# Four graph layers on one core: the slot's order changed at its seam and in its middle

## The reference

```python
x = _layernorm(x + L0(x, adj))   # conv1 -> relu -> conv2 (17 taps) -> + x -> relu
                                 # s = x @ w_se.T + b_se;  A = exp(-dist(s)) * adj
                                 # x_nmp = A @ relu(x @ w_msg.T + b_msg);  GRU(x_conv, x_nmp; x)
x = _layernorm(x + L1(x, adj))   # A = adj * sigmoid(q k^T / sqrt(128));  D^-1/2 A D^-1/2 X
x = _layernorm(x + L2(x, adj))   # tangent = artanh(|x|) x/|x|;  s = adj @ tangent
                                 # s * min(tanh|s|, 0.996) / |s|
x = _layernorm(x + L3(x, adj))   # relu(D^-1/2 (adj + I) D^-1/2 (x W^T + b) * mask)
```

## Time and profile before

| | |
|---|---|
| median of 3 runs | 797.41 us (796.39 to 798.12) |
| the profiled execution | 798.0 us, of which its span (first to last instruction) is 796.2 |
| busy share of the span | PE 90%, PEld 68%, DVE 79%, ACT 53%, POOL 17% |
| mean granted TensorE clock | 0.964 of full |
| one full slot | 45.30 us |

### The profile page before, as it was taken

One profiled execution on the slowest core, in us unless ns is written; L12 is line 12 of the kernel. 1 busy time (PEld: TensorE's weight loads), 2 busy tenths in 40 slices (PEclk: granted clock), 3 DMA queues, 4 the chain that ended last, 5 costly groups with the idle time before them and its releaser, 6 DMA issues.

```text
span 796.2 us, 12758 instructions
## 1 busy us (share of the span) xinstructions
PE 715.7 (90%) x3984; PEld 542.6 (68%) x3984; DVE 625.2 (79%) x2080; ACT 424.7 (53%) x881; POOL 135.3 (17%) x151
## 2 busy tenths in 40 slices
PE   3889999999999999999999999999999999998653
PEld 1766777777676877767776777767677776765531
DVE  7456788888878887888888888887888888876655
ACT  4164737556473755657373755647374655624431
POOL 0000111211122111211121121121121121111221
PEclk8889999999999999999999999999999999999776
DMA  5303241150605133060514224060423215101000
GB/s 198 119 14 129 97 158 68 57 169 14 224 14 171 66 108 116 23 215 13 193 44 162 75 66 158 13 224 13 171 66 122 102 45 192 54 14 54 0 14 27
DMA packets 46586, 75.33 MB, mean 95 GB/s; under 512 B 4065, under 2 KB 12769, under 8 KB 46433
## 3 DMA queue, kind: packets, MB, share of 16 engines
q1 hardware_dynamic: 46560, 75.02, 27.6%
HBM read 70.82 MB, written 4.19 MB: 94 GB/s over the span
## 4 chain that ended last, share of the span: by engine, by line
DVE 40%; PE 36%; issue 11%; ACT 9%; POOL 3%; DVEq 1%; DMA 0%; SPq 0%; ACTq 0%; POOLq 0%
PE K L1400 7%; DVE BIG L751 5%; PE C L1292 4%; PE CONV L1266 4%; DVE A L824 4%; PE F L1292 3%; ACT X L414 2%; DVE X L692 2%; POOL RSTD L336 2%; DVE Z L866 2%; ACT L553 2%; PE F L1353 2%; DVE FS L926 2%; DVE Z L991 2%; DVE ST L668 2%
## 5 line engine op out<-in xcount | busy, mean ns | idle before, releaser
L336 POOL TENSOR_TENSOR RSTD<-VEPS,POW 128x4 f32<-128x4 f32 x48 | 48.8, 1017 | 341.6 <-DVE VEPS L686 341.6
L1266 PE MATMUL CONV<-H1H,WH 128*128 128x256 f32 x288 | 85.6, 297 | 0.0
L1266 PE MATMUL CONV<-H1L,WH 128*128 128x256 f32 x288 | 81.4, 283 | 0.0
L1266 PE MATMUL CONV<-H1H,WL 128*128 128x256 f32 x288 | 81.2, 282 | 0.0
L1400 PE MATMUL K<-ADJR,FS 128*128 128x512 f32 x112 | 52.9, 617 | 10.1 <-DVE FS L926 10.1
L1364 PE MATMUL C<-QT,KT 128*128 128x512 f32 x128 | 61.6, 606 | 0.1
L1232 PEld LDWEIGHTS K<-XS,BIG 128*128 128x128 f32 x496 | 57.8, 192 | 1.3
L1232 PE MATMUL K<-XS,BIG 128*128 128x128 f32 x496 | 57.9, 275 | 0.0
L1232 PEld LDWEIGHTS K<-FX,ADJR 128*128 128x128 f32 x448 | 51.1, 192 | 9.9 <-issue 8.2
L1372 PE MATMUL F<-A,MSG 128*128 128x512 f32 x128 | 57.5, 592 | 0.0
L1266 PEld LDWEIGHTS CONV<-H1L,WH 128*128 128x128 f32 x288 | 55.2, 192 | 0.0
(11 more groups left out here) (251 smaller groups left out, 1932.1 us busy)
## 6 DMA issues: line engine op xcount, KB each, us to landing
ADJF<-in_adjT SPq DMA_DIRECT2D x16, 1024.0 KB, 5.3
ADJN<-in_adj SPq DMA_DIRECT2D x16, 1024.0 KB, 7.7
ADJM<-in_adjT SPq DMA_DIRECT2D x15, 1024.0 KB, 6.9
ADJR<-in_adjT SPq DMA_DIRECT2D x14, 1024.0 KB, 5.2
X_IN<-in_xT SPq DMA_DIRECT2D x16, 256.0 KB, 2.6
out<-OUT SPq DMA_DIRECT2D x16, 256.0 KB, 3.2
BIG<-in_weights SPq DMA_DIRECT2D x1, 1088.0 KB, 5.4
BIG<-in_weights SPq DMA_DIRECT2D x1, 576.0 KB, 8.7
```

Of the source, the lines that this page charges most:

```text
L336: nc.gpsimd.tensor_tensor(RSTD[:, row, :], VEPS[:, row, :], POW[:, 0, :], ALU.pow).then_inc(ev[f"ln{layer}_rstd"], 1)
L1266: last = mm(out, w[:, at_col + k * P:at_col + (k + 1) * P], h[:, k:k + PH], start=(k == 0 and i == 0), stop=(k == count - 1 and i == 2))
```

## The change

The distances get a bank each and move behind the transposes and the message rows; the bank list `DB` replaces the alternation, so F1 and K1 are used as well, and the transposes of Y move to F0, the message rows to K0.

```diff
+        DB = (C0, C1, F1, K1)
...
         def support_bank(n, c):
-            return (K0 if n["last"] else K1) if c < C // 2 or not n["drain"] else F0
+            return (K0 if n["last"] else K1) if c < C // 2 else F0 if n["drain"] else C1
...
             def support_norms(n):
                 for c in range(C):
-                    act.wait_ge(ev["agg2_done"], nth(finished(n, c), n["r"]))
+                    act.wait_ge(ev["agg2_done"], nth(c | 1, n["r"]))
...
+            def distances(n):
+                pe.wait_ge(ev["str_ready"], n["f"])
+                pe.wait_ge(ev["w_ready"], n["f_prev"])
+                pe.wait_ge(ev["gate_u"], n["f_prev"])
+                pe.wait_ge(ev["r_ready"], n["f_prev"])
+                pe.wait_ge(ev["res_scaled"], n["r_prev"])
+                for c in range(C):
+                    mm(DB[c][:, :], cols(STL, c), STR[:, :], start=True, stop=True).then_inc(ev["dist_done"], 1)
...
             def state_by_nodes(n):
                 pe.wait_ge(ev["y_ready"], n["m"])
-                pe.wait_ge(ev["d_kept"], n["m_prev"])
-                pe.wait_ge(ev["str_ready"], n["f"])
-                for c in range(C):
-                    last = nc.tensor.transpose(cols(K0, c), cols(Y, c), IDENT[:, :])
+                pe.wait_ge(ev["gate_t"], n["m"])
+                for c in range(C):
+                    last = nc.tensor.transpose(cols(F0, c), cols(Y, c), IDENT[:, :])
```

TensorE's `body` (in a full slot):

```diff
-                distances01(n)
                 if mid:
                     state_by_nodes(n)
-                distances23(n)
-                messages(n)
+                    messages(n)
+                distances(n)
...
                 if rear:
                     support(n)
+                summed_messages(n)
                 sum_taps(n)
                 odd_taps(8, EVEN).then_inc(ev["conv2_done"], 1)
-                summed_messages(n)
                 own_gates(n)
+                reset_gate_of_x(n)
+                if rear:
+                    last_aggregation(n)
                 if mid:
                     attention_degree(n)
-                reset_gate_of_x(n)
-                if rear:
-                    last_aggregation(n)
+                if rear:
+                    last_linear(n)
                 gates_of_messages(n)
-                if rear:
-                    last_linear(n)
                 reset_gate_of_conv(n)
```

More of the change, by code:

```diff
@@ L1177, in ending @@
                 degree_guard(c)
+                norm_guard(c)
                 ball_factor(c)
@@ L1256, in _ @@
             first_conv(1, 0)
-            factors(1, 0, 0)
+            factors(1, 0)
             own_squares(1)
@@ L1294, in gate @@
                 return done
-            def distances(c):
-                mm(CB[c % 2][:, :], cols(STL, c), STR[:, :], start=True, stop=True).then_inc(
-                    ev["dist_done"], 1)
+            def distances(n):
[4 more added lines that the diff above has]
+                pe.wait_ge(ev["res_scaled"], n["r_prev"])
+                for c in range(C):
+                    mm(DB[c][:, :], cols(STL, c), STR[:, :], start=True, stop=True).then_inc(ev["dist_done"], 1)
             def first_taps(n):
@@ L1351, in projections @@
                 mm(query_bank(n)[:, :], plain(F_Q), X1T[:, :], start=True, stop=True).then_inc(ev["q_done"], 1)
+                pe.wait_ge(ev["x1_ready"], every(n["m"]))
+                mm(F0[:, :], plain(F_K), X1T[:, :], start=True, stop=True).then_inc(ev["k_done"], 1)
                 pe.wait_ge(ev["msg_sum"], n["f"])
-                mm(F0[:, :], plain(F_K), X1T[:, :], start=True, stop=True).then_inc(ev["k_done"], 1)
                 rows_of(K0, X1T, plain(F_LIN)).then_inc(ev["x_done"], 1)
@@ L1384, in attention_degree @@
                 pe.wait_ge(ev["asum_ready"], n["m"])
-                pe.wait_ge(ev["x_raw"], n["m"])
-                pe.wait_ge(ev["xconv_part"], n["f"])
+                pe.wait_ge(ev["q_raw"], n["m"])
+                if n["drain"]:
+                    pe.wait_ge(ev["z1_ready"], every(n["m_prev"]))
                 for c in range(C):
-                    last = mm(K0[:, c:c + 1], cols(ASUM[:, 2, :], c), ONES[:, :], start=True, stop=True)
+                    last = mm(K2[:, c:c + 1], cols(ASUM[:, 2, :], c), ONES[:, :], start=True, stop=True)
                 last.then_inc(ev["wdeg_done"], 1)
@@ L1438, in body @@
                 following = not isinstance(t, int) or t + 1 < B
-                distances01(n)
                 if mid:
                     state_by_nodes(n)
-                distances23(n)
-                messages(n)
+                    messages(n)
+                distances(n)
+                if not mid:
+                    messages(n)
                 first_taps(n)
@@ L1457, in body @@
                     support(n)
+                summed_messages(n)
                 sum_taps(n)
                 odd_taps(8, EVEN).then_inc(ev["conv2_done"], 1)
-                summed_messages(n)
                 own_gates(n)
-                if mid:
-                    attention_degree(n)
                 reset_gate_of_x(n)
@@ L1466, in body @@
                     last_aggregation(n)
-                gates_of_messages(n)
+                if mid:
+                    attention_degree(n)
                 if rear:
                     last_linear(n)
+                gates_of_messages(n)
                 reset_gate_of_conv(n)
                 if following:
-                    factors(n["f_next"], n["m"], n["f"])
+                    factors(n["f_next"], n["f"])
                     first_conv(n["f_next"], n["f"])
@@ L1494, in ending @@
                 support(a)
+                summed_messages(a)
                 sum_taps(a)
                 odd_taps(8, EVEN).then_inc(ev["conv2_done"], 1)
-                summed_messages(a)
                 own_gates(a)
+                reset_gate_of_x(a)
+                last_aggregation(a)
                 attention_degree(a)
-                last_aggregation(a)
-                reset_gate_of_x(a)
                 gates_of_messages(a)
```

131 lines of the change are left out of this document (74 added, 57 removed).

## The result

The changed kernel takes 773.25 us (median of 4 runs, 771.02 to 774.81), the kernel before 797.76 on the same chip (4 runs): a ratio of 0.9688, 95% interval 0.9654 to 0.9722, or 24.5 us less. The forecast was 782, with a range of 774 to 791: direction and places were right, but the gain is half as large again as the 16.1 us of the prediction's sum, and the time lies just under the range.

A forecast was written before the change was run, and what follows sets the result against it. TensorE was taken to bound the kernel, with only gaps between its products to gain. Seam 0.46 plus middle 0.74 less 0.05 made 1.15 us in 14 slots, 16.1 off 798.0, forecast 782 us, range 774 to 791.

The forecast's parts named there:

- the 16.1 us of the prediction's sum: Whole kernel: 0.46 at the seam plus 0.74 in the middle less 0.05, 1.15 us in each of 14 slots.
- the seam: TensorE's stretch from `attended` to the first convolution tap, 6.30 us; gain forecast up to Q's projection 0.46 us a slot.
- XT leaves Y's path, 0.61: VectorE at the seam: XT moves from between STR and NG, so Y starts 0.61 us earlier.
- Y's end to the first transpose is now 0.25; kept: TensorE at the seam: transposes of Y start 0.25 us after Y's end, taken as unchanged.
- X1 is done before TensorE's taps; that wait goes: Seam: X1 ends at 456.38, taps at 456.64, so TensorE's 1.05 us wait before X1's transposes goes.
- ScalarE is late next, and 0.7 comes back at X1T: Seam: X1T ends at 458.82 without idling, so TensorE waits about 0.7 us before the projection of Q.
- the rival in which ScalarE is not late: Exponentials follow faster or start sooner; seam gives 1.19, slot 1.88, 26 us in all, time 771; chance 0.08.
- The wait for FS goes: TensorE ahead of `last_aggregation`: wait falls from 0.78 to 0.04 us, gain 0.74, without slack.
- The middle is worth 0.69: Second aggregation to `last_aggregation`: 0.74 us a slot from the FS wait, less 0.05 for the copy behind.
- a loss of cover alone: Behind `last_aggregation`: its sums' copy is covered by degree products (0.89), formerly six split products (1.40); 0.05 us lost.
- 1.15 "in each of 14 full slots": Slot gain 1.15 us times 14, 16.1; partial gains of first slots set against losses in the ending.
- A rule against the change: Semaphore reads at 50 to 100 ns for five added TensorE waits: 0.25 to 0.5 a slot, time 785 to 789.

The follow-up runs named there:

- xt_behind: Changed kernel with XT put back behind STL and STR on VectorE, as before the change; ratio 0.9805, slot 44.35 us.
- stats_ahead: Changed kernel with the four statistics of Z1 put back ahead of X1 on VectorE; ratio 0.9700, slot 43.74 us.
- degrees_first: Changed kernel with ScalarE's four row sums of ADJN moved ahead of the four exponentials; ratio 0.9614, slot 43.34 us.
- old_ending: Changed kernel; in the last full slot alone, `last_aggregation` again ahead of the reset gate's products, behind the degree products, VectorE's middle in former order; ratio 0.9735.
- third_wait: Changed kernel with one more, long fulfilled wait (for STR) ahead of the transposes of Y on TensorE; ratio 0.9707, slot 43.81 us.
- five_waits: Changed kernel with five more fulfilled waits on TensorE, three ahead of the distances, two ahead of the second aggregation's second half; ratio 0.9691.
- y_wait_last: Kernel before the change, with the three waits of the transposes of Y reordered: STR, kept degrees, Y last; ratio 0.9998, slot 45.20 us.
- sums_behind: degrees_first with `sum_of_h1` on VectorE moved behind `tangent`; ratio to the kernel before 0.9659, slot 43.43 us.

## Why the prediction came out too high, step by step

Times at the seam are counted from the start of `attended`.

- *XT leaves Y's path, 0.61.* Right: Y ended at 3.72, forecast 3.71, and xt_behind gave the 0.61 back.
- *"Y's end to the first transpose is now 0.25; kept."* This step failed. It was 0.05. The 0.25 was read from a slot of the loop as a constant of the handoff, but it held only there, where the wait for Y stood on an instruction of its own with another wait between it and the transposes; in the changed kernel the weight load carries it. In the written-out slots it had been 0.05 before, and the two full ones ahead of the loop gave 1.27 and 1.29 where the loop's gave 1.56. The transposes started at 3.77 instead of 3.96, and from there to Q it took 7.38 where the forecast had 7.43: together the 0.24 by which the seam was undersized (0.70 against 0.46).
- *X1 is done before TensorE's taps; that wait goes.* Right: X1 ended at 8.84, forecast 8.85. But stats_ahead shows that taking the statistics off its path earned nothing as long as ScalarE is late.
- *ScalarE is late next, and 0.7 comes back at X1T.* Right: X1T without idling at 10.49 (10.69 forecast), and 0.66 more between X1's transposes and Q. degrees_first shows that it is ScalarE's list. So the rival in which ScalarE is not late came near in time, 771, for another reason than its own.
- *The wait for FS goes.* Right, but the working left 0.04 of it and no slack, and there is 0.28. VectorE took up T 1.95 after the second aggregation, not 2.24: GpSimd's power started at 0.90 and took 1.01 where the working had 1.00 and, from one row of before, 1.21; and from Z to FS's end it was 5.30 for 5.39.
- *The middle is worth 0.69.* Undersized: 0.89 in the slot in view. Beside the wait (0.78) TensorE itself needed 0.17 less up to `last_aggregation`: without wait and degree products 8.75 us for 8.92. That is the size of two changes from plain products to split ones that the new order spares there: one behind the second aggregation (471.47 to 471.68, 0.21 where split taps follow each other at 0.12) and one behind the degree products (480.41 to 480.73, 0.32 for 0.23). This is read from the rows; no run took it apart. The forecast moved the second along with the degree products, so that it counted as no gain, and saw the change of order as a loss of cover alone (0.05; 0.08 was lost). The rows of the kernel before behind the first and ahead of the second:

```profile
471.68 0.28 PE L1266 MATMUL K<-HSL,WH 128*128 128x256 f32 x1
...
480.41 0.48 PE L1292 MATMUL F<-XH,WH 128*128 128x512 f32 x1
```

- *1.15 "in each of 14 full slots"*, with start and ending set against each other. This step failed too. The last full slot, which stands in the ending, gave 3.18, not 1.15: there the wait for FS had been 1.83 and `last_aggregation` behind it slow. old_ending brought both back. Of the start and the tail, taken as nothing together, the tail gave 0.94; why is open.
- *A rule against the change.* Five fulfilled waits cost nothing, so the 785 to 789 was wrong here. The Trainium skill (Advanced Engine Details and Errata, Miscellaneous Facts, Network/Comms) gives 50 to 100 ns for a sequencer's reading of a semaphore. In the loop of third_wait the instruction that carries the late wait ahead of the weight load goes with 0.08 to 0.09 us, which agrees in size; by five_waits long fulfilled waits cost nothing that shows.

In numbers: 16.1 was forecast for 14 slots. Thirteen gave 20.0 (0.39 more each, 5.1 in all), the last one 2.0 more than its 1.15, and start and tail 1.0: 24.2. The sum's last step has a slip of its own: 781.9 less 0.6 is 781.3 and not 781.5, which decides nothing.

## What to carry to other kernels

When a gap closes, look for the list that is late next on every engine: here the row sums on ScalarE, then the power on GpSimd, then the sigmoids, each hidden behind the last, and each worth moving only after the one before. A handoff taken from a row holds for the instructions that stand in it: look which one carries the late wait and what stands between it and the work, in the loop and outside it, and leave waits fulfilled long before out. Read the first and the last slots by themselves: a wait there can be more than twice that of a full slot (1.83 for 0.62), and the slower products behind it come on top.

## What the runs showed of the hardware

- TensorE's transposes start 0.05 to 0.06 us after the late Y where their weight load carries the wait (the changed kernel), 0.13 to 0.14 where an instruction just ahead of it does (third_wait's loop, y_wait_last), and 0.24 to 0.25 where one more stands between (the loop of the kernel before). Five more fulfilled waits changed a slot of 43.73 us by 0.01.
- A wait of 1.83 us (the kernel before) and one of 1.59 us (old_ending), behind 0.94 us of one-column products in an else busy stretch, were followed by products partly at the lower clock level (granted clock 0.67 and 0.65): eight took 4.65 and 4.74 us instead of 3.11, so the wait cost about twice its length.
- From the first Y to the second 38.41, 37.03 and 35.62 us passed in the profiled executions of the kernel before, the changed one and sums_behind; the granted clock of that stretch was 0.93, 0.95 and 1.00. The kernels differ there too, so the clock's own part isn't known. Totals that differ by less than 2 us are better told apart by the slot.
